# The decayed-scan input `u` of a two-layer gated attention kernel: made by GpSimd instead of VectorE

## What is computed

```python
x = x + tanh(g_xattn[0]) * L0_xattn(layernorm(x), ctx)   # 16 heads, softmax over 256 context rows and a null key
x = x + tanh(g_ffn[0])   * L0_ffn(layernorm(x))          # two matmuls, fp8-rounded hidden values
x = x + tanh(g_xattn[1]) * L1_xattn(layernorm(x), ctx, lens)
x = x + tanh(g_ffn[1])   * L1_ffn(layernorm(x))          # top 2 of 8 experts
```

```python
h = rmsnorm(embeds, g_res) @ W_in + b_in
h_patch = rmsnorm(patch_embeds, g_init)[..., :256]
s[p] = exp(-dt) * s[p-1] + exp(logp) * h_patch[p]
out = s[plug[token]] + h
```

## Time and profile before

| | us |
|---|---|
| median of 3 runs | 1618.31 |
| lowest and highest | 1617.9 and 1618.65 |
| the profiled execution | 1617.25 |
| its span, first to last instruction | 1615.5 |
| TensorE busy | 1464.1 (91%) |
| VectorE busy | 1201.5 (74%) |
| ScalarE busy | 923.2 (57%) |
| GpSimd busy | 624.8 (39%) |

### The profile page before, as it was taken

The page is one execution under the profiler, slowest core; times in us unless marked ns, Lnnn a source line. Parts: engine busy times, 40 slices in busy tenths (PEclk is TensorE's granted clock), DMA queues, the critical chain, the costliest instruction groups (busy, mean ns, idle before and its releaser), DMA issues.

```text
span 1615.5 us, 36153 instructions
## 1 busy us (share of the span) xinstructions
PE 1464.1 (91%) x12542; PEld 1078.1 (67%) x12542; DVE 1201.5 (74%) x3263; ACT 923.2 (57%) x2526; POOL 624.8 (39%) x762
## 2 busy tenths in 40 slices
PE   3789999999999999999999999999865399999997
PEld 2566776767677676767777677777644266666665
DVE  5478898898989888898989889898873354455443
ACT  4276767767676776767676676767651133333332
POOL 4011324424342433434243342424333355555554
PEclk8899999999999999999999999999887699999999
DMA  8102020210202021120202022010500373333332
GB/s 245 64 21 66 2 80 15 66 67 15 79 2 80 12 69 42 40 80 2 80 2 79 14 66 79 3 60 2 177 14 20 96 189 54 56 56 60 58 60 31
DMA packets 77599, 92.90 MB, mean 58 GB/s; under 512 B 21248, under 2 KB 61200, under 8 KB 77424
## 3 DMA queue, kind: packets, MB, share of 16 engines
q1 hardware_dynamic: 50912, 72.69, 13.7%
q0 software_dynamic: 15680, 17.78, 6.7%
q10 hardware_dynamic: 10832, 0.13, 0.4%
HBM read 60.70 MB, written 30.78 MB: 57 GB/s over the span
## 4 chain that ended last, share of the span: by engine, by line
PE 53%; DVE 31%; ACT 9%; issue 3%; SPq 2%; DMA 1%; POOL 1%; ACTq 0%; POOLq 0%; DVEq 0%
PE S L1305 11%; PE W L970 8%; PE W L972 8%; PE W L971 8%; DVE mx L1490 6%; PE O L1325 6%; PE T L975 5%; ACT prob L805 4%; DVE pTl L1502 3%; PE O L1074 3%; PE S L1048 2%; PE W L975 2%; DVE st_ln L1461 1%; ACT prob L814 1%; DVE xh L1471 1%
## 5 line engine op out<-in xcount | busy, mean ns | idle before, releaser
L805 ACT ACTIVATE prob<-S,nm 128x256 f32<-128x256 f32 x512 | 236.0, 475 | 81.1 <-DVE nm L1493 80.9
L641 POOL TENSOR_SCALAR ve_ln<-mv_ln 128x2 f32<-128x2 f32 x64 | 14.4, 225 | 568.3 <-DVE mv_ln L1464 568.2
L798 ACT ACTIVATE pTh<-T 128x512 f16<-128x512 f32 x256 | 139.3, 596 | 109.5 <-PE T L975 109.3
L1305 PE MATMUL S<-GL,xgh 128*128 x568 | 170.1, 381 | 2.8 <-DVE xgl L1794 2.8
L1502 DVE SCALAR_TENSOR_TENSOR pTl<-T,pTh 128x512 f16<-128x512 f32 x256 | 163.8, 680 | 6.9 <-ACT pTh L798 6.9
L1490 DVE TENSOR_REDUCE mx<-S 128x2 f32<-128x512 f32 x256 | 163.0, 677 | 7.5 <-PE S L1048 7.5
L735 POOL DMA_INDIRECT out_dram<-ysb,tab x71 | 112.2, 1580 | 132.1 <-issue 90.6
L814 ACT ACTIVATE prob<-prob,rden 128x256 f32<-128x256 f32 x256 | 116.2, 501 | 70.6 <-DVE p0n L1511 70.5
L975 PE MATMUL T<-ident,prob 128*128 128x128 f32 x1024 | 142.0, 283 | 1.8 <-DVE prob L1517 1.7
L970 PE MATMUL W<-cTh,Wkh 128*128 128x256 f16 x512 | 140.8, 275 | 0.0
L972 PE MATMUL W<-cTh,Wkl 128*128 128x256 f16 x512 | 140.6, 275 | 0.0
(11 more groups left out here) (301 smaller groups left out, 4358.8 us busy)
## 6 DMA issues: line engine op xcount, KB each, us to landing
cx<-in_ctx_dram SPq DMA_DIRECT2D x16, 512.0 KB, 5.1
gst<-in_L_ffn_gating_w_dram SPq DMA_DIRECT2D x16, 512.0 KB, 6.1
gating_split<-gsp SPq DMA_DIRECT2D x16, 512.0 KB, 2.7
GL<-gating_split SPq DMA_DIRECT2D x8, 1024.0 KB, 5.2
stg<-in_L_xattn_Wkv_dram SPq DMA_DIRECT2D x8, 512.0 KB, 13.6
xl<-in_x_dram SPq DMA_DIRECT2D x16, 256.0 KB, 4.3
lst<-in_L_ffn_linear_w_dram SPq DMA_DIRECT2D x16, 256.0 KB, 5.2
xres<-in_x_dram SPq DMA_DIRECT2D x16, 256.0 KB, 2.7
```

What stands on the lines that cost most here:

```text
L798: A(flat(pTh[:, h, :, :]), T[h][:, :], ACT.Copy).then_inc(s_pTh[h], 1)
L805: ins = A(prob[:, h, t, :], S[h][:, t * NTOK:(t + 1) * NTOK], ACT.Exp, bias=nm[:, h, t:t + 1], scale=SM, accum_out=rs[:, h, t:t + 1])
L1305: ins = M(o[:, :], (xgl if n == 2 else xgh)[i % 2][:, k, :], GLflat[:, bass.ds(w, HID)], start=(k == 0 and n == 0), stop=(k == KD - 1 and ...
```

## The change

The two VectorE instructions that make `u` of batch `nxt` are taken out of `j = 7`, with the waits for `rc` and for the last split. GpSimd makes `u` instead, right behind its split of the batch in work: two `tensor_scalar` (context times `rc`), a wait for them, two `tensor_tensor` (times `gi_b`, in place). One more linked instruction makes `POOL_STEPS` 16. GpSimd thus makes `u` early in step `i` and splits it early in step `i+1`.

```diff
-POOL_STEPS = 15
+POOL_STEPS = 16
...
                     link(pool.tensor_copy(uh[i.par][:, :, :], u[:, :, :]))
                     pool.tensor_tensor(ul[i.par][:, :, :], u[:, :, :], uh[i.par][:, :, :], ALU.subtract)\
                         .then_inc(s_us, 1)
+                if PRE in parts:
+                    wait_apart(pool, s_rstd["ctx"], nxt.n + 1)
+                    at_least(pool, s_us, nxt.n)
+                    for t in range(TT):
+                        ins = pool.tensor_scalar(u[:, t, :], cx[nxt.par][:, t, 0:D], rc[:, t:t + 1], None, ALU.mult)
+                    link(ins)
+                    for t in range(TT):
+                        ins = pool.tensor_tensor(u[:, t, :], u[:, t, :], gi_b[:, :], ALU.mult)
+                    ins.then_inc(s_u, 1)
                 if POST in parts:
                     rstd_of("ln2", post, 1e-5).then_inc(s_rstd["ln2"], 1)
...
                         if pre:
-                            dve.wait_ge(s_rstd["ctx"], nxt.n + 1)
-                            at_least(dve, s_us, nxt.n)
-                            for t in range(TT):
-                                ins = V.scalar_tensor_tensor(u[:, t, :], cx[nxt.par][:, t, 0:D], rc[:, t:t + 1],
-                                                             gi_b[:, :], ALU.mult, ALU.mult)
-                            ins.then_inc(s_u, 1)
-                        if pre:
                             v_low(2)
                             v_low(3)
```

## The result

| | before | with the change |
|---|---|---|
| median of 5 runs, us | 1618.24 | 1625.0 |
| lowest and highest, us | 1615.82, 1618.65 | 1623.77, 1626.1 |
| ratio | | 1.0044 [1.0029, 1.0058] |
| span of the profiled execution, us | 1615.5 | 1622.0 |
| `lg` of one batch to `lg` of the next, us | 71.51 | 72.12 |

The change makes the kernel 0.44% slower, 6.8 us. The forecast was 1623.2. The page's first part answers to the earlier trace rows: VectorE has 32 instructions and 2 us less, GpSimd 64 instructions and 53 us more.

The account below looks back on a forecast made before the run. The last stage was taken as bound by TensorE, then ScalarE's `vh` and `pTh`, then VectorE's `pTl`. 1617.25 + 0 + 4.9 = 1622.2 us profiled, with 1.06 for the median 1623.2; range 1617 to 1630.

Parts of the forecast that it names:

- The removal is worth nothing: In the last stage, dropping VectorE's two `u` instructions (0.79 us) gains nothing, since `pTl` still waits for ScalarE's `pTh`.
- (a): Sign in the last stage: `vl` from about 563.95, split by a wait for `vh`, and `pTl` still waiting for `pTh`.
- GpSimd's 3.3 us fit into its idle 3.71: Behind `ul`, GpSimd's four new instructions take 3.3 us (ends 2.5 and 3.4) of 3.71 idle, delaying nothing queued behind.
- One hold of the second `x`: GpSimd's first `tensor_tensor` gets in ahead of VectorE's second `x` and holds it 0.4 us per batch; chance 0.40.
- Nothing else is held: The `tensor_scalar` cost `p0n` and `prob` nothing, and the second `tensor_tensor` runs beside the one-input statistics at no cost.
- The slack of 0.05: In front of `values`, 0.05 us per batch of VectorE's loss goes unpaid; an estimate from two gaps.
- The sum: Per batch 0.4 us held less 0.05 is 0.35, over 14 steps 4.9 us: 1622.2 profiled, 1623.2 median.
- Point (d): Sign: the interval between batches goes from 71.5 us to 71.85; below 71.4 or above 72.3 would prove the prediction wrong.
- the first (they miss each other): The second `x` asks for the port before GpSimd's first `tensor_tensor`, which costs nothing: 1618.3 us; chance 0.35.
- The second rival (two held): Two VectorE instructions are held per batch (both `x`, or the statistics): 0.75 us, 1628.8 us in all; chance 0.13.
- The third (the whole instruction): GpSimd holds VectorE for its whole instruction, at `p0n`, `prob` and `x`: 1.75 us per batch, 1642.8 us; chance 0.05.
- The fourth (VectorE bounded the last stage): VectorE's queue bounded the last stage, so 0.5 to 0.8 us per batch come back: 1607 to 1611 us; chance 0.07.

Follow-up runs that it names:

- experiment 1: Changed kernel with GpSimd's four `u` instructions cut to two columns and `u` filled once with a constant: 1617.2 us, ratio 1.0000 to the kernel before.
- experiment 4: Changed kernel with only the two `tensor_tensor` cut to two columns: 1619.78 us; then with only the `tensor_scalar` cut, the `tensor_tensor` reading the context: 1626.35 us.
- experiment 6: Changed kernel with GpSimd's two `tensor_tensor` moved behind the reciprocal root of `ln2`, nothing cut: 1619.24 us, ratio 1.0017 to the kernel before.

## Why the prediction was right

By its steps:

- *The removal is worth nothing.* Right, and shown alone (1.0000 [0.9991, 1.0008]). The first `vl` came 0.80 earlier, the second at the same time, and the wait of 0.29 for `pTh` stayed, as (a) said.
- *GpSimd's 3.3 us fit into its idle 3.71.* Right in outcome, short in size. The `tensor_scalar` take 0.93 us each and not 0.85 (1.93 for the pair), the `tensor_tensor` 0.73 alone as the earlier trace rows have it, and the start comes 0.19 behind `ul` instead of 0.1: 3.6 us in all. GpSimd was left 0.57 us of idle time in front of `ve_ln`, in a stretch that itself had become longer. Nothing behind it was late.
- *SyncE's load.* It cost nothing: experiment 1, in which `s_u` comes just as early, has the time of the kernel before.
- *One hold of the second `x`.* The mechanism and the place are right, seen in the rows and taken away by itself in experiments 4 and 6. The size was a little low: 0.48 instead of 0.40.
- *Nothing else is held.* This step was wrong. I put the first `tensor_scalar` past `p0n` and the second behind the second `prob`, at no cost. They cost 0.03 and 0.13, together 0.16, and with the `tensor_tensor` cut away 0.14 of distance stay. The slip was to give `prob` the path without comparing starts: the second `prob` ran while GpSimd's first instruction gave way to its second, so it was not there first. Which of the two held it, the rows don't tell.
- *The slack of 0.05.* Right in size, wrong in place. In front of `values` there was none: 0.64 of longer instructions started `values` 0.65 later. The 0.04 was won back behind it, and the distance grew by 0.61.
- *The sum.* 0.35 per batch predicted, 0.61 measured; 4.9 us predicted, 8.2 measured over the full steps. The steps, the start and the expert phase together give 8.6 us against the 4.9 of the forecast. That the forecast of 1623.2 stands only 1.8 us from the median of 1625.0 is therefore in part luck. In the profiled executions the last two steps gave back 2.1 us at a higher granted clock, which no step of the sum had, and medians of so few executions are not known to better: the interval of the ratio goes from 4.7 to 9.4 us and holds both sums. Point (d) named 71.85 as the distance and 72.3 as the bound of its own failure; 72.12 is nearer to the second.

Of the rivals, the first (they miss each other) fell, and its turning point was wrong. It said that a `tensor_scalar` of 0.93 us would let `x` go first. The price was 0.93, and they met. The 0.19 and the hold of `prob` moved both engines: the `tensor_tensor` started at 589.46, the second `x` at 589.50. It was a matter of 0.04 us, so a chance of 0.35 for this rival was not too much, and experiment 6 shows that such a miss is to be had by moving two instructions. The second rival (two held) fell: the statistics with one input took 0.75 beside the second `tensor_tensor`, as before. The third (the whole instruction) fell too: a hold of 0.48 to 0.52 stands against 0.73 for the instruction. The fourth (VectorE bounded the last stage) fell with experiment 1.

Not settled: which of the two `tensor_scalar` held `prob`, and why the clock in the last two steps differs. It differs between executions that do the same work there, and no run here takes it apart.

## What to carry to other kernels

Before you move work to GpSimd, look at what runs beside it on VectorE. Here instructions that read PSUM and the statistics went on unheld. Instructions with two SBUF inputs were held, and so was a one-input `tensor_scalar` from SBUF. Behind a `tensor_tensor` of 256 columns a hold cost about 0.5 us even if the held instruction had four columns. So lay the two timelines over each other at the new place before counting the time saved. Look first for the idle time of the engine that has the work: here 2.8 us of waiting stood in another stage of the same step, and using it, with the statistics moved into the place that came free, made the kernel 0.7% faster with no other engine touched. And when a removed instruction only lengthens the next wait, see what else could fill that wait before giving the move up or calling it done.

## What the runs showed of the hardware

- A hold is shorter than the GpSimd instruction that causes it: 0.48 to 0.52 us for a `tensor_tensor` of 256 columns that takes 0.73. Where `x` and `prob` were held they started 0.04 and 0.01 us behind it, so both came free some 0.53 us after its start (for `prob` the records are those of experiment 4); `d` started 0.10 behind it and came free at 0.59. The Trainium skill's page "SBUF — State Buffer" says that the pair is held for the whole instruction; the measurement decides here.
- GpSimd instructions that only write held a `tensor_scalar` with one input by 0.35 us, until 0.40 us after their start. Instructions with two SBUF inputs lost nothing beside them: `x` and `p0n` 0.36 and 0.34 us into a write, and one `den` 0.11 us into one.
- The statistics (`BATCH_NORM_STATS2`, one input) took 0.75 us beside a reading `tensor_tensor`, the same as with GpSimd idle.
- On GpSimd a multiplication of 256 columns by one value per partition takes 0.93 us with one operation, while the same kind of instruction with two operations takes 0.48.
- The granted clock of TensorE in the last two steps stood at 0.86 and 0.70 in one profiled execution and at 0.90 and 0.74 in another with the same work there. The two steps differed by 2.1 us, a third of the 6.5 us between the two spans.
